# Scatter phase: pairs innermost in the transposition buffers, and the gathered sums taken from PSUM by VectorE

## What is computed

```python
grouped = x.reshape(b, s // 32, 32, d)                    # groups of 32 tokens
perm = (logits == max over the 32 tokens of the group)    # each expert picks one token of each group
permuted = einsum('bntd,bntes->bnesd', grouped, perm)     # gather: the picked token of each expert
inner = relu(einsum('bnesd,esdf->bnesf', permuted, W1) + b1)            # 512 -> 32
result_permuted = einsum('bnesf,esdf->bnesd', inner, W2) + b2           # 32 -> 512
result = einsum('bnesd,bntes->bntd', result_permuted, perm)             # scatter back to the tokens
```

## Time and profile before

| | us |
|---|---|
| median of 3 runs (lowest, highest) | 3041.65 (3038.51, 3043.23) |
| the profiled execution | 3036.95 |
| its span in the trace | 3035.2 |
| busy over the span: PE, DVE, ACT, POOL | 2799.8, 2220.8, 1749.4, 1628.4 |
| mean granted TensorE clock | 0.973 of full |

### The profile page before, as it was taken

One profiled execution on the slowest core, in us unless ns is written; L12 is line 12 of the kernel. 1 busy time (PEld: TensorE's weight loads), 2 busy tenths in 40 slices (PEclk: granted clock), 3 DMA queues, 4 the chain that ended last, 5 costly groups with the idle time before them and its releaser, 6 DMA issues.

```text
span 3035.2 us, 135365 instructions
## 1 busy us (share of the span) xinstructions
PE 2799.8 (92%) x59836; PEld 2250.2 (74%) x59836; DVE 2220.8 (73%) x2743; ACT 1749.4 (58%) x3552; POOL 1628.4 (54%) x2447
## 2 busy tenths in 40 slices
PE   8999999999999999999999999996878868887877
PEld 6888888888888888888888888875667754444443
DVE  6777777777777777777777777774444449999998
ACT  5665666666666566665666656653333335565654
POOL 4666766766667676666666766761101104344434
PEclk9999999999999999999999999998999979998988
DMA  4222222222222222222222222226544435566554
GB/s 152 74 75 74 76 74 77 77 79 70 71 78 74 78 76 73 76 74 77 77 73 76 74 73 78 72 59 211 142 130 124 114 127 172 176 201 202 175 173 137
DMA packets 262713, 316.38 MB, mean 104 GB/s; under 512 B 28000, under 2 KB 184032, under 8 KB 260464
## 3 DMA queue, kind: packets, MB, share of 16 engines
q1 hardware_dynamic: 252176, 297.55, 32.2%
q10 hardware_dynamic: 9952, 10.17, 1.0%
HBM read 194.31 MB, written 113.31 MB: 101 GB/s over the span
## 4 chain that ended last, share of the span: by engine, by line
PE 87%; issue 6%; DVE 4%; DMA 1%; SPq 1%; POOL 1%; ACT 0%; POOLq 0%; ACTq 0%; DVEq 0%
PE a_proj L991 39%; PE a_mix L991 11%; PE s_ps L1719 6%; PE g_pick_ps L1465 5%; PE a_scan L1105 5%; PE s_ps L1740 5%; PE s_ps L1735 3%; DVE g_picked L1394 3%; PE a_scan L1082 3%; PE a_scan L1069 2%; PE g_acc_ps L1489 2%; PE a_mix L1057 2%; PE a_misc L1049 1%; PE a_misc L1123 1%; DMA part_dram<-res 1%
## 5 line engine op out<-in xcount | busy, mean ns | idle before, releaser
L1700 DVE STREAM_TRANSPOSE s_turned<-s_stage 128x2048 f32<-128x2048 f32 x128 | 539.0, 5225 | 2.0 <-ACT s_stage L1678 2.0
L991 PE MATMUL a_proj<-wdh,xTh 128*128 128x512 f32 x1024 | 421.6, 412 | 6.0 <-issue 4.2
L991 PE MATMUL a_proj<-wdh,xTl 128*128 128x512 f32 x1024 | 402.5, 393 | 0.0
L991 PE MATMUL a_proj<-wdl,xTh 128*128 128x512 f32 x1024 | 401.3, 392 | 1.2 <-issue 1.2
L823 DVE COPY_PREDICATED scan_in<-mask,a_scan 64x512 f32<-64x512 uint32 x512 | 382.3, 747 | 16.1
L1678 ACT COPY s_stage<-s_ps 128x1024 f32<-128x1024 f32 x256 | 247.1, 1018 | 210.5 <-DVE s_turned L1700 107.6
L472 POOL TENSOR_TENSOR yv<-yt,dx 128x512 f32<-128x512 f32 x128 | 189.2, 1478 | 292.2 <-DVE yt L863 292.2
L464 POOL TENSOR_TENSOR dx<-xs,d_row 64x512 f32<-64x512 f32 x256 | 331.5, 1295 | 15.1
L1657 POOL TENSOR_TENSOR s_out<-s_out,s_part 128x512 f32<-128x512 f32 x128 | 164.8, 1288 | 325.6 <-ACT s_out L1684 324.5
L639 ACT ACTIVATE scan_in<-CT,hsel 64x128 f32<-64x128 f32 x1024 | 326.1, 388 | 4.8
L603 ACT ACTIVATE raw<-a_proj,rs 128x272 f32<-128x272 f32 x128 | 62.5, 489 | 427.8 <-PE a_proj L991 427.8
(11 more groups left out here) (153 smaller groups left out, 7362.7 us busy)
## 6 DMA issues: line engine op xcount, KB each, us to landing
x<-in_x_dram SPq DMA_DIRECT2D x128, 256.0 KB, 2.6
xn_dram<-xn SPq DMA_DIRECT2D x128, 256.0 KB, 2.4
part_dram<-res SPq DMA_DIRECT2D x128, 256.0 KB, 2.5
g_xn<-xn_dram SPq DMA_DIRECT2D x512, 64.0 KB, 2.2
s_part<-part_dram SPq DMA_DIRECT2D x128, 256.0 KB, 3.6
out_dram<-s_out SPq DMA_DIRECT2D x128, 256.0 KB, 2.9
xr<-in_xT_dram SPq DMA_DIRECT2D x126, 256.0 KB, 2.9
s_inner<-inner_dram SPq DMA_DIRECT2D x32, 512.0 KB, 5.3
```

Of the source, the lines that this page charges most:

```text
L991: last = nc.tensor.matmul(out, lhs[a], rhs[c], start=(k == 0 and n == 0), stop=(k == nk - 1 and n == 2))
L1700: nc.vector.transpose(turned[m % 2][:, :, cols].rearrange("p n d -> p d n"), stage[m % 2][:, :, cols].rearrange("p e d -> p d e")).then_in ...
```

## The change

Two things are changed in the scatter phase, with no other phase touched.

First, `stage` and `turned` get another order of the free axes: two neighbouring experts (or groups) lie side by side as the innermost axis, behind the column, so that each side of a transposition walks over pairs of 8 bytes with 2048 bytes between pairs. ScalarE's eviction then writes every second element (8 bytes apart), and TensorE's matmul at L1740 streams its 256 columns 8 bytes apart. The shapes and numbers of all these instructions stay.

Second, copy_out (ScalarE) and the add (GpSimd) go, with their semaphore `out_cp`. VectorE does one operation in their place: it reads the sums from PSUM and `part` from SBUF and writes `out`. These adds stand behind the transpositions in VectorE's list: transposition y of step m, then the add of unit y of step m-1. GpSimd is left with `spread_perm` alone.

```diff
-    stage = [sb(f"stage{i}", [P, EX // 4, DH], at=a) ...
-    turned = [sb(f"turned{i}", [P, SG, DH], at=AT_PICKED + 32768 * i) for i in range(2)]
+    stage = [sb(f"stage{i}", [P, EX // 8, DH, 2], at=a) ...
+    turned = [sb(f"turned{i}", [P, SG // 2, DH, 2], at=AT_PICKED + 32768 * i) for i in range(2)]
...
-        spread_perm(0)
-        for v in range(UNITS):
-            m, x = divmod(v, QB)
-            pool.wait_ge(out_cp, v + 1)
-            pool.wait_ge(part_in[v % NPART], 16 * (v // NPART + 1))
-            nc.gpsimd.tensor_tensor(out[v % NOUT][:], out[v % NOUT][:], part[v % NPART][:], ALU.add).then_inc(out_add, 1)
-            if x == 0 and m + 1 < STEPS:
-                spread_perm(m + 1)
+        for m in range(STEPS):
+            spread_perm(m)
...
-        places = stage[m % 2][:, 8 * i:8 * i + 8, :].rearrange("p (j r) d -> p r j d", r=4)
+        places = stage[m % 2][:, 4 * i:4 * i + 4, :, :].rearrange("p (j h) d r -> p h r j d", h=2)
         for h in range(2):
-            nc.scalar.copy(places[:, 2 * h:2 * h + 2, :, :], bank[:, pair(u, h), :, :]).then_inc(w2_cp, 1)
+            nc.scalar.copy(places[:, h, :, :, :], bank[:, pair(u, h), :, :]).then_inc(w2_cp, 1)
...
-        def copy_out(v):
-            act.wait_ge(out_ps, v + 1)
-            wait(act, out_done[v % NOUT], 16 * (v // NOUT))
-            nc.scalar.copy(out[v % NOUT][:], bank[:, 6 + v % 2, :, :]).then_inc(out_cp, 1)
...
     def vector_program(dve):
+        def add_part(v):
+            dve.wait_ge(out_ps, v + 1)
+            dve.wait_ge(part_in[v % NPART], 16 * (v // NPART + 1))
+            wait(dve, out_done[v % NOUT], 16 * (v // NOUT))
+            nc.vector.tensor_tensor(out[v % NOUT][:], bank[:, 6 + v % 2, :, :], part[v % NPART][:], ALU.add).then_inc(out_add, 1)
+
         for m in range(STEPS):
             dve.wait_ge(w2_cp, 2 * QB * (m + 1))
             wait(dve, out_ps, QB * (m - 1))
             for y in range(4):
                 cols = slice(DT * y, DT * y + DT)
-                nc.vector.transpose(turned[m % 2][:, :, cols].rearrange("p n d -> p d n"),
-                                    stage[m % 2][:, :, cols].rearrange("p e d -> p d e")).then_inc(turn_cp, 1)
+                nc.vector.transpose(turned[m % 2][:, :, cols, :].rearrange("p n d i -> p d n i"),
+                                    stage[m % 2][:, :, cols, :].rearrange("p e d i -> p d e i")).then_inc(turn_cp, 1)
+                if m > 0:
+                    add_part(QB * (m - 1) + y)
+        for v in range(UNITS - QB, UNITS):
+            add_part(v)
...
-            wait(pe, out_cp, v - 1)
+            wait(pe, out_add, v - 1)
...
-                                            turned[m % 2][:, g * (SG // GPT) + 2 * x + t, :], start=False, stop=True,
+                                            turned[m % 2][:, g * (SG // GPT // 2) + x, :, t], start=False, stop=True,
```

More of the change, by code:

```diff
@@ L1539, in scatter_phase @@
     w2 = sb("w2", [P, QB, 8, DH], at=AT_W1)
-    stage = [sb(f"stage{i}", [P, EX // 4, DH], at=a) for i, a in enumerate((AT_XNT, AT_W1 + 32768))]
-    turned = [sb(f"turned{i}", [P, SG, DH], at=AT_PICKED + 32768 * i) for i in range(2)]
+    stage = [sb(f"stage{i}", [P, EX // 8, DH, 2], at=a) for i, a in enumerate((AT_XNT, AT_W1 + 32768))]
+    turned = [sb(f"turned{i}", [P, SG // 2, DH, 2], at=AT_PICKED + 32768 * i) for i in range(2)]
     inner = [sb(f"inner{i}", [P, NQ, SG], at=a) for i, a in enumerate((AT_PERM1, AT_PERM0, AT_XN3 + 12288))]
@@ L1563, in scatter_phase @@
     out_ps = sem("out_ps")
-    out_cp = sem("out_cp")
     out_add = sem("out_add")
@@ L1675, in evict @@
         wait(act, turn_cp, 4 * (m - 1))
-        places = stage[m % 2][:, 8 * i:8 * i + 8, :].rearrange("p (j r) d -> p r j d", r=4)
+        places = stage[m % 2][:, 4 * i:4 * i + 4, :, :].rearrange("p (j h) d r -> p h r j d", h=2)
         for h in range(2):
-            nc.scalar.copy(places[:, 2 * h:2 * h + 2, :, :], bank[:, pair(u, h), :, :]).then_inc(w2_cp, 1)
+            nc.scalar.copy(places[:, h, :, :, :], bank[:, pair(u, h), :, :]).then_inc(w2_cp, 1)
     def scalar_program(act):
-        def copy_out(v):
-            act.wait_ge(out_ps, v + 1)
-            wait(act, out_done[v % NOUT], 16 * (v // NOUT))
-            nc.scalar.copy(out[v % NOUT][:], bank[:, 6 + v % 2, :, :]).then_inc(out_cp, 1)
         for i in range(2):
             act.wait_ge(gat["inner_out"][i], gat["inner_count"] * (NGB // 2))
[L1688 to L1692, removed]
-    def vector_program(dve):
+        for u in range(4, UNITS):
+            evict(act, u)
+    def vector_program(dve):
+        def add_part(v):
[3 more added lines that the diff above has]
+            nc.vector.tensor_tensor(out[v % NOUT][:], bank[:, 6 + v % 2, :, :], part[v % NPART][:], ALU.add).then_inc(out_add, 1)
         for m in range(STEPS):
```

## The result

| | before | after |
|---|---|---|
| median of 4 runs (lowest to highest of the comparable ones), us | 3040.08 (3037.68 to 3043.23) | 2924.57 (2918.12 to 2926.86) |
| profiled execution / its span, us | 3036.95 / 3035.2 | 2926.86 / 2925.1 |
| granted TensorE clock, mean | 0.973 | 0.988 |

The ratio is 0.9612, with a 95% interval of 0.9591 to 0.9634: 3.9% faster. The forecast was 2904 us with a range of 2890 to 3010, so the direction and the mechanism held and the gain was forecast too large: 138 us, where the two profiled executions differ by 110.

What follows compares the result with a forecast made beforehand. VectorE was taken as the bound, TensorE next. Against the profiled 3036.95 us: 138.4 less to the last transposition, 1.2 less tail, 2 more for W2's reload, giving 2899.3; plus 4.7 for the median, 2904 us. Range 2890 to 3010, own range 2895 to 2920.

Steps and rivals of the forecast that it cites:

- VectorE was the bound, and TensorE is late next: Scatter phase: VectorE, busy 50.00 us in 50, sets 16.85 us a step; TensorE's own pace is 12.36 us a step.
- The transpositions at 2.31 us: VectorE's transpositions in the pair layout: from 4.213 us each down to 2.31 us, the lower bound.
- Rival 1: VectorE's transposition does not gain; VectorE stays the bound and carries 84.9 us of adds: 3125 us, chance 0.15.
- rival 2: VectorE's transposition gains half, 3.22 us, each pair costing three cycles; VectorE is the bound: 3002 us, chance 0.11.
- The add at 0.69 us, hidden: VectorE's added sums: 0.69 us each; unit 2.31 + 0.69 = 3.00 us, below TensorE's 3.09, waits costed at nothing.
- ScalarE and TensorE at no extra cost: ScalarE's writes and TensorE's stream of `turned`, now 8 bytes apart, were each taken to cost nothing more.
- rival 3: TensorE's stream or ScalarE's writes run at half pace, plus 1.07 us a unit: 3030 us, chance 0.10.
- 118 x 3.09 = 364.6: Time in us from the apply of unit 9 to that of unit 127, at TensorE's 3.09 us a unit.
- Start: unchanged: Start of the scatter phase: evictions 4 to 7 unchanged, the last ending at 2499.03 us as in the profiled execution.
- the tail: End of the kernel behind the last transposition, 13.7 us before: the last add ends 1.2 us sooner.

## Why the prediction was right, and where its size was off

- **VectorE was the bound, and TensorE is late next**: right, by the stretches and the waits. With VectorE out of the way the clock is granted in full.
- **The transpositions at 2.31 us**: right, 2.302. The reason given (stalls on addresses far apart, not a fixed rate of two cycles) is borne out by the runs with one side and with four. Rival 1, no gain, and rival 2, half the gain at 3.22 us, fell. The reason given for rival 2, that reads and writes pay in turn, is half true: each side alone costs 1.4 or 1.5 us and both together 2.0.
- **The add at 0.69 us, hidden**: right, 0.689, with 0.22 us of slack in the unit where 0.09 had been reckoned, since successive instructions overlap a little. Without the layout it cost 65 us and not the 84 of rival 1, for the same reason.
- **ScalarE and TensorE at no extra cost**: nearly. The eviction costs 130 ns more and is not on the path. The gather records cost 0.04 us more and are: a unit is 3.134 and not 3.09 us, 118 x 0.044 = 5.2 us. The price that rival 3 set, a doubling, is real, but in these runs it comes with a step of 16 bytes and not of 8.
- **"118 x 3.09 = 364.6"** is the term that failed. The units took 383.4 us: 5.2 more for the gather records, 13.6 more for pauses and the waits at the reload. The forecast had put 2 us there, for the reload alone, and had taken two quiet units of the kernel before for the rule. The profile that the forecast used shows no such pause in any unit, so they could not be read from it: they came with the faster pace. The start was 1.1 and the tail 0.9 us better than reckoned: 5.2 + 13.6 - 2 - 1.1 - 0.9 = 14.8 of the 14.9 us.
- **"Start: unchanged"** was right as a statement on the change and wrong as an anchor: 12.7 us of the miss is that one execution before had begun early. The forecast added 4.7 us for the median over the profiled one; the start alone wanders by more.
- **The adds themselves** are worth some 9 us on top of the layout (2931.4 against 2922.5), which the forecast had at 1.2, the tail; why, stays open. Taken to the phase, layout and adds together give 121.4 us: from 536.0 to 414.6.

## What to carry to other kernels

When an engine at 50 of 50 is relieved, the next one's pace should be measured over a long stretch and not over two good units: this TensorE lost 13.6 us, most of it in pauses of which the slower kernel's profile showed none. A layout change of a transposition brings most of its gain only when made on both of its sides, and should go no further than the neighbours can follow: two fp32 side by side were right here, four took the gain away again. And a sum against one profiled execution should be made from a point inside the changed phase, with the wander of what lies ahead kept in the range.

## What the runs showed of the hardware that was not expected

- The start of the last phase wanders by 12.7 us between executions of one unchanged kernel (2480.5 and 2493.2 us), while the phase itself repeats within 0.3 us in that kernel and 2.4 us in the changed one.
- From start to start, a transposition of 128x2048 with one side in single elements 1024 bytes apart takes 3.65 or 3.75 us, with both sides 4.18, with neither 2.22. Recorded lengths of instructions that follow each other without a gap hold an overlap: in the kernel before the median recorded is 5.3 us, where the next one starts after 4.20.
- ScalarE writing and TensorE streaming fp32 lose 13% and 4% at a step of 8 bytes, and a factor of 1.8 to 2 at 16 bytes (1017, 1148 and 2095 ns; 1.07, 1.11 and 2.00 us).
- TensorE pauses for 0.3 to 3.1 us in the middle of a run of matmuls that has no wait in it, 5 to 14 times in 118 units at 3.13 us a unit, and at most once where a unit takes 4.0 us or more. Every pause ends 1.2 to 1.6 us behind the end of a 16 KB transfer of the instruction queue, and most stand at the same matmuls in every kernel. Leaving out the part loads, about a third of the phase's bytes, brought them from 9 to 3 us.
- Behind a pause of 2 us the granted clock can fall to 0.50 for 3.4 us (five times in the run where ScalarE copies), and it can stay at 1.00 (behind 1.96 us in the changed kernel).
